# Second layer: the products with values of a head pair in one group behind the items, spread by transposes, and one wait less

## What is computed

```python
# kind 1: latent attention
q = (x @ Wq.T).reshape(b, t, 8, 64)
kv_latent = x @ Wkv_down.T
k = (kv_latent @ Wk_up.T).reshape(b, t, 8, 64)
v = (kv_latent @ Wv_up.T).reshape(b, t, 8, 64)
attn = softmax(einsum('bqhd,bkhd->bhqk', q, k) * scale)
x = x + einsum('bhqk,bkhd->bqhd', attn, v).reshape(b, t, 512) @ Wo.T
# kind 2: attention whose values and outputs are mixed by gates, 2 of 5 experts each
wv = topk_mask(x @ Ws, 2) * sigmoid(x @ Ws)
v = einsum('bthe,btek->bhtk', wv, einsum('btd,edk->btek', x, Wv))
attn = einsum('bhij,bhjd->bihd', softmax(q @ k.T * scale), v)
x = x + einsum('bthe,bthk,ekd->btd', topk_mask(x @ Wd, 2), attn, Wo)
```

## Time and profile before

| what | value |
|---|---|
| median of 3 runs | 2932.53 us (2927.82 to 2939.71) |
| span of the profiled execution | 2945.6 us |
| PE busy over the span | 2437.2 us (83%) |
| DVE, ACT, POOL busy | 1901.8, 1690.7, 1929.2 us |
| PE, products with values (L1581) | 278.3 us in 1024 instructions |
| PE, scores (L1552) | 292.1 us in 1024 instructions |
| PE, transposes of probabilities (L1563) | 275.4 us in 2048 instructions |

### The profile page before, as it was taken

One profiled execution on the slowest core, in us unless ns is written; L12 is line 12 of the kernel. 1 busy time (PEld: TensorE's weight loads), 2 busy tenths in 40 slices (PEclk: granted clock), 3 DMA queues, 4 the chain that ended last, 5 costly groups with the idle time before them and its releaser, 6 DMA issues. The chain is left out here.

```text
span 2945.6 us, 31726 instructions
## 1 busy us (share of the span) xinstructions
PE 2437.2 (83%) x10259; PEld 1143.9 (39%) x10259; DVE 1901.8 (65%) x3077; ACT 1690.7 (57%) x2384; POOL 1929.2 (65%) x1920
## 2 busy tenths in 40 slices
PE   5667777777877777764988999999999999999995
PEld 2222323332323232232555444444444444444442
DVE  4798989898979897821333564656556564656554
ACT  0678888888888889920221545454444544454351
POOL 5455587877777778856775018575657475764776
PEclk8668787878787877776999999999999999999998
DMA  2000000000100000163996000000000100000000
GB/s 99 6 9 1 17 15 17 15 17 15 15 17 15 17 8 17 17 111 66 284 268 154 14 1 1 1 15 8 15 8 1 22 1 22 1 8 1 8 1 14
DMA packets 92452, 98.99 MB, mean 34 GB/s; under 512 B 20320, under 2 KB 88032, under 8 KB 92256
## 3 DMA queue, kind: packets, MB, share of 16 engines
q1 hardware_dynamic: 66544, 69.80, 8.9%
q0 software_dynamic: 25712, 26.90, 4.7%
HBM read 69.98 MB, written 26.67 MB: 33 GB/s over the span
## 5 line engine op out<-in xcount | busy, mean ns | idle before, releaser
L948 POOL TENSOR_TENSOR TT<-TT,SS 128x512 f32<-128x512 f32 x512 | 651.9, 1309 | 216.3 <-ACT SS L877 215.8
L1648 ACT ACTIVATE PR<-S,NM 128x512 f32<-128x512 f32 x512 | 347.6, 684 | 492.5 <-DVE NM L1816 492.3
L1816 DVE TENSOR_REDUCE NM<-S 128x2 f32<-128x1024 f32 x256 | 313.1, 1223 | 293.0 <-PE S L1552 292.2
L700 DVE TENSOR_SCALAR TT<-SC 128x1024 f32<-128x1024 f32 x256 | 311.7, 1218 | 80.2 <-POOL TT L948 44.7
L447 PE MATMUL OB<-TT,VAL 128*17 128x512 f32 x1024 | 343.8, 774 | 4.8 <-ACT TT L885 4.8
L953 POOL DMA_INDIRECT slot_tokens<-TID,IDX x256 | 260.0, 1016 | 130.6 <-issue 79.6
L702 DVE SCALAR_TENSOR_TENSOR SS<-SC,TT 128x1024 f32<-128x1024 f32 x256 | 313.6, 1225 | 20.6 <-issue 1.8
L1581 PE MATMUL OT<-TT,VN 128*64 128x512 f32 x1024 | 278.3, 622 | 20.5 <-ACT TT L1654 16.7
L1552 PE MATMUL S<-TT 64*128 64x512 f32 x1024 | 292.1, 646 | 0.7 <-ACT TT L1617 0.7
L1563 PEld LDWEIGHTS TP<-ident,PR 128*128 128x128 f32 x2048 | 226.9, 141 | 149.7 <-issue 121.0
L1563 PE MATMUL TP<-ident,PR 128*128 128x128 f32 x2048 | 275.4, 277 | 10.1 <-DVE TT L1821 8.7
(11 more groups left out here) (272 smaller groups left out, 4168.6 us busy)
## 6 DMA issues: line engine op xcount, KB each, us to landing
TT<-w_gu SPq DMA_DIRECT2D x64, 384.0 KB
TT<-w_dn SPq DMA_DIRECT2D x64, 128.0 KB
XL<-x SPq DMA_DIRECT2D x8, 512.0 KB
rows<-XL SPq DMA_DIRECT2D x8, 512.0 KB
slot_tokens<-TID,IDX POOLq DMA_INDIRECT x256
TT<-w_dn SPq DMA_DIRECT2D x64, 64.0 KB
XS<-stream SPq DMA_DIRECT2D x8, 512.0 KB, 3.8
out<-XS SPq DMA_DIRECT2D x8, 512.0 KB, 2.9
```

Of the source, the lines that this page charges most:

```text
L700: dve.tensor_scalar(tt[:, :, mt, :], SC[mt % 2][:], 0.0, None, ALU.max)
L948: ins = pool.tensor_tensor(tt, tt, ss, ALU.add)
L1648: act.activation(PR[s % 2][h2][:], S[s % 2][:, h2, :], ACT.Exp, bias=NM[:, s % 2, h2:h2 + 1], accum_out=SM[:, pair % 2, j, h2:h2 + 1]).the ...
L1816: dve.tensor_reduce(NM[:, s % 2, :], S[s % 2][:], AX, ALU.max, negate=True).then_inc(sems["peak"], 1)
```

## The change

Three edits of PE's program in stage three; no other engine's instructions change.

1. `attend` of a pair is called for all four key tiles in one step, the one in which only key tile 0 stood before (s % 4 == 0), and behind the items of slots 2 to 4 instead of ahead of them. In the other three steps of four PE has no products with values.
2. Of the waits of key tile 0, that for both copies of the current step stays only for the last pair of all.
3. `spread` uses `transpose` instead of a matmul with the identity as the moving operand.

```diff
                 for j in range(NT):
-                    ins = pe.matmul(bank[:, j * P:(j + 1) * P],
-                                    RB[:, 2 * j:2 * j + 2, :].rearrange("p h d -> p (h d)"), ident[:], start=True, stop=True)
+                    ins = pe.transpose(bank[:, j * P:(j + 1) * P],
+                                       RB[:, 2 * j:2 * j + 2, :].rearrange("p h d -> p (h d)"), ident[:])
...
-            def attend(v, r, pair, m):
+            def attend(v, r, pair, m, last):
...
-                    for way in "da":
-                        if v.all_due("in_" + way):
-                            pe.wait_ge(sems["in_" + way], v.value)
+                    if last:
+                        for way in "da":
+                            if v.all_due("in_" + way):
+                                pe.wait_ge(sems["in_" + way], v.value)
...
+                carry(v, parts, r, s, 2, 3, 4)
                 rr, pair = behind(r, s)
-                if rr >= 0 and rr < TAIL and (r < TAIL or s < NT):
-                    attend(v, rr, pair, s % NT)
-                carry(v, parts, r, s, 2, 3, 4)
+                if rr >= 0 and rr < TAIL and s % NT == 0 and (r < TAIL or s < NT):
+                    for m in range(NT):
+                        attend(v, rr, pair, m, r == TAIL)
```

## The result

The changed kernel is slower: a median of 2958.15 us over six runs (2950.52 to 2967.31) against 2935.49 us for the kernel before (2927.82 to 2944.59), a ratio of 1.0076 with a 95% interval of 1.0051 to 1.0101. The forecast was 2930.5, 2 us under the 2932.53 of the three runs that it started from, with a range up to 2951. Within the six runs the time goes with the mean granted clock of TensorE: 2950.52 us at 0.885, 2967.12 us at 0.872.

What follows compares the result with a forecast made beforehand. PE was taken to set the pace until 2700 us, POOL after. Seven pairs of runs gave about 0 and the tail -1.5, rounded to -2 us: span 2945.6 to 2943.6, median forecast 2930.5 us, range 2906 to 2951.

Steps and rivals of the forecast that it cites:

- The clock: Rival, chance 0.03: in steps without products PE's clock falls behind waits, +130 us, time 3060.
- The walk of a full pair: Pair of runs in stage three: waits rise from 8.2 to 14.0 us, +5.8, saved PE work -5.8, so about 0.
- The three bare places: Transposes before steps 8, 12 and 15 of kind 2, no item between: each loses 0.8 us, 2.4 a run.
- Before step 4 of kind 1: Transposes there, behind statistics on DVE, would wait 1.9 us for DVE's copy of TP.
- the experts: Experts' items in steps 7 and 8 of kind 1: their wait grows from 1.31 to 2.0 us.
- the gates: Gates item in step 6 of kind 1, behind DVE's copy RB: wait taken as 1.0 us, before 0.55.
- The spread by transposes: Four transposes instead of matmuls save 0.53 us of PE a spread, four spreads in a pair of runs.
- The dropped wait: Key tile 0's wait for two copies cost 16.7 and 2.8 us; little of this comes back as time.
- Small waits: Rival, chance 0.28: only the three places without items wait longer; a pair is 3.4 us shorter, time about 2907.
- POOL's additions: Rival on the slower side, chance 0.18: DVE meets them more often, +2.8 us a pair of runs, time about 2951.
- No gain in a row: Rival, chance 0.05: grouped products still cost 1.01 us each, 24.5 us are missing, time 2955.
- The tail: Behind 2700 us POOL has the pace; only an earlier `heads2` and the last groups count, -1.5 us.

Runs made afterwards that it cites:

- the kernel with another tail: Changed kernel, but with one key tile of products a step and the wait kept in the last two runs of the stage; ratio to the kernel before 1.0095.
- The filling experiment: Changed kernel with matmuls that compute nothing put where PE waits, ahead of the second experts' item and behind `heads2`; ratio to the kernel before 1.0034.
- the second profile of the changed one: Changed kernel measured again without any edit, on another chip's baseline; ratio to the kernel before 1.0069, eleven falls in the five full pairs.

## Why the prediction was wrong

- **The clock: the step that failed.** The sum had no term for it, and as a rival it had a chance of 0.03 and a price of +130 us. The chance came from one sentence, that no expected wait is over 2.5 us and that the stretch ran at full clock with its transposes. Waits far below 2.5 us were enough, two of them with little work between (1.30 and 0.84; 0.70 and 1.85), or a single one of 1.85. My own walk contained all three places. I had priced each new wait by its own length alone. And the price was wrong the other way: I let one step without products in three run at half clock, while in the two profiles there are none to three falls a pair, which together cost up to 3.6 us, 12 us in the five full pairs of the first profile. With one or two falls of 1.7 us in each of seven pairs the rival would have stood at about 2942 to 2954, and with a real chance.
- **The walk of a full pair: right in its sum, less so in its terms.** +5.8 and -5.8 us were to cancel, and without falls a pair takes 160.4 us as before, in the changed kernel's own first full pair and in the three of the kernel with another tail. But the waits shown there are 11.7 us together, not 14.0 (before 8.2), and PE's busy time fell by 4.0 us (152.1 to 148.1), not 5.8. A part of both gaps is the way of counting (busy time holds the ends of instructions ahead of a wait, which distances from start to start leave out); how much of them is errors that happen to cancel is not shown. A small slip: a pair is 160.4 us long, not about 154, with nine waits, not eight; the 8.2 us are right for it. The parts: a group from its start to the transposes behind it takes 2311.59 - 2308.01 = 3.58 us, as summed. The three bare places wait for ACT's copy, 0.44 us shown and about 0.2 ahead of the first half, where I had 0.8. Before step 4 of kind 1 the wait is 1.85 (I had 1.9), for the experts 1.85 and 0.70 (2.0 and, in the slower rival, 0.8), `heads2` 1.30 and 1.04 (2.5 in all), the gates 0.64 (1.0).
- **The spread by transposes: 1.5 us a pair alone**, not 2.1. Of the rest, 0.4 us is the experts' wait, which grew from 1.3 to 1.7.
- **The dropped wait: a gain of 1.2 us a pair alone**, where I had said little of it comes back. Spread and dropped wait together are worth 2.7 us a pair by their own runs, and the grouping alone loses 1.6 at full clock and more with its falls. My sum held the same in it (8 x 0.46 saved against nearly all of the new waits); I did not draw from it that the grouping is the part to leave out. The three don't add up in the pair: -1.5 - 1.2 + 1.6 = -1.1, measured 0 (160.4 without falls). Why is not shown.
- **Small waits: did not come.** The waits of L1563 in a pair are 2.5 + 1.3 = 3.8 us shown, not under 2.5.
- **POOL's additions: did not come.** RB takes 0.45 us (median) and never over 0.90, and it was this that should have decided the rival:

```profile
L1832 DVE COPY RB<-RS x32: 427/448/898, 1637.5 to 2751.5; 128x512 f32<-128x512 f32 x32
```

  Its number, 2951, lies near the measured one by luck: its reason did not occur. The same holds for the 2955 of the next rival.
- **No gain in a row: did not come.** 16 instructions in 3.65 us.
- **The start of the stage: a term that was missing.** I counted seven pairs alike at 0. The stretch from the second `latent` item to the third, mostly in the two runs of kind 1 that follow each other, has few waits before (3.6, 0.9, 0.3 and 0.2 us) and so little to give back; it became 3.4 us longer (154.6 to 158.0). Its wait of 0.9 us became 2.3, that of 3.6 became 4.5, and new are 2.3 us for DVE's copy, 1.5 and 1.0 for ACT's copy XV and 1.0 for AT. The clock is 0.98 in both kernels there. The stretch from the first item to the second became 2.3 us longer (33.1 to 35.4), with clocks of 1.00 and 0.95.
- **The tail: -1.5 expected, +10.3 found** (mine began at 2700 us, this one with the last `latent` item). 27.4 us more of it lie under full clock (62.7 against 35.3). Counted only where PE worked, and at half speed, this is 14.7 us, more than the whole +10.3, so part of it did not reach the end. The last products alone lost 5.9 us; what the falls ahead of them cost at the end no row shows. That it is the clock, the rows make likely; that it is due to this change, they do not show, since the kernel with the old tail has it too, and so has the one with the dropped wait alone.

Summed, the clock accounts for 12 us in the five pairs, up to 10.3 in the tail and about 1 at the start, so for up to 23 of the 29.4 us of stage three; the other 6 or so are waits, most of them at the start. The filling experiment moved the median by 0.35 to 0.42% of 2954 us, 10 to 12 us, as the part of it in the pairs would have it. For the tail no run parts this change from chance.

## What to carry to other kernels

Where PE sets the pace at full clock, do not price a new wait by its length alone. Look for places where a wait of 1 or 2 us is new or two waits have come close together: the work behind can take twice as long, in some executions and not in others, so give such a place a cost and a chance. Here it was up to 3.6 us a pair. Work taken off PE and turned into waits was worth nothing here, so group only as far as the next engine's copy is still covered (here two tiles ahead of the items, and neither four nor two behind the items), and try the edits of one change apart. Work that computes nothing, put into such a wait, is a quick test for this cost, and here it was itself a gain over the changed kernel, though not over the kernel before.

## What the runs showed of the hardware

- A stretch in which PE was busy for 2.19 of 4 or 2.34 of 4.5 us, with no wait over 1.85 us, was followed by half clock for about 3.4 us. In an execution of the kernel with another tail, whose instructions are the same up to there, the same stretches (2.18 of 4, 2.33 of 4.5) were not, nor was one with 2.40 of 4 us in the kernel before. The single wait of 1.85 us was not followed by a fall at 2345.89, but it was in the filled kernel (2200.40) and in the second profile of the changed one. So the program makes a fall possible, and does not fix it. I had not expected that with waits this short.
- Half clock can stay while PE works without a pause: 12 of 12 us from 2942.50 in the changed kernel. What would have ended it no run shows.
- Of the products with values, a tile's four instructions cost 1.01 us alone and 0.855 behind others of their form, 0.155 less; the group of four gave 3.58 us as that predicts. What takes the 0.155 us no run shows.
- With all spreads as transposes, beside the transposes of every step, the kernel before had no fall from 1750 to 2700 us: that PE did transposes did not bring the clock down there.
